# Attention and weight statistics of a four-stage layer kernel: twelve chunk buffers, sums on VectorE, low parts and bias on GpSimd

## The reference, cut to what matters

```python
x = x + _L0_attn_ref(_layernorm(x), Wqkv, bqkv, Wo, bo)
x = x + _L0_ffn_ref(_layernorm(x), w1, mean_w1, w2, mean_w2, w3, mean_w3)
# _L0_attn_ref
qkv = x @ Wqkv + bqkv                      # 512 -> 3 * 128
attn = softmax(q @ k.T / sqrt(128))
out = (attn @ v) @ Wo + bo
# _L0_ffn_ref, each of its three weights is replaced by
d = w - mean_w
W = mean_w + mean(abs(d)) * sign(d)
h = silu(x @ W1.T) * (x @ W3.T);  out = h @ W2.T
```

## Time and profile before

| what | us |
|---|---|
| median of 3 runs | 1560.31 (1559.79 to 1561.89) |
| the profiled execution: its own time | 1560.82 |
| its span from first to last instruction | 1558.9 |
| first stage: up to the first `weff` | 165.16 |
| PE busy over the span | 1348.8 (87%) |
| DVE, ACT, POOL busy | 1146.0, 827.5, 655.3 |

### The profile page before, as it was taken

The page is one execution under the profiler, slowest core; times in us unless marked ns, Lnnn a source line. Parts: engine busy times, 40 slices in busy tenths (PEclk is TensorE's granted clock), DMA queues, the critical chain, the costliest instruction groups (busy, mean ns, idle before and its releaser), DMA issues.

```text
span 1558.9 us, 21230 instructions
## 1 busy us (share of the span) xinstructions
PE 1348.8 (87%) x7142; PEld 1123.2 (72%) x7142; DVE 1146.0 (74%) x2233; ACT 827.5 (53%) x1794; POOL 655.3 (42%) x620
## 2 busy tenths in 40 slices
PE   2875899999778898779465999999999999999977
PEld 1753688888677876667244888888888888888866
DVE  5544433323438899789987999998888998889864
ACT  3575322223225665566333777667766667667741
POOL 3433000000027664555333655555555555666612
PEclk9966799999989999999566999999999999999998
DMA  6543000000021135545650000000000000000011
GB/s 217 170 154 117 0 1 0 1 1 1 11 85 57 53 104 161 161 133 149 201 173 30 12 1 26 26 26 26 26 27 26 26 26 26 26 26 15 12 64 54
DMA packets 83723, 95.59 MB, mean 61 GB/s; under 512 B 11681, under 2 KB 59297, under 8 KB 83105
## 3 DMA queue, kind: packets, MB, share of 16 engines
q1 hardware_dynamic: 83616, 94.24, 19.3%
HBM read 75.34 MB, written 18.87 MB: 60 GB/s over the span
## 4 chain that ended last, share of the span: by engine, by line
PE 65%; DVE 13%; issue 3%; ACT 2%; POOL 2%; DMA 2%; SPq 2%; DVEq 1%; POOLq 0%; ACTq 0%
PE ps L311 15%; PE ps L313 15%; PE ps L312 15%; PE ps L1561 8%; PE ps L1581 3%; PE ps L1580 3%; DVE xn_l L1238 2%; DVE rop L1196 2%; DMA wuvo<-pr_hl 1%; DVE rop L1194 1%; DVE acc L1173 1%; PE ps L1352 1%; DVE pm L1226 1%; PE ps L1473 1%; DVE rop L1195 1%
## 5 line engine op out<-in xcount | busy, mean ns | idle before, releaser
L652 POOL TENSOR_SCALAR pm<-pm,smx 128x128 f32<-128x128 f32 (+7 forms) x256 | 190.2, 752 | 212.1 <-DVE smx L1232 212.1
L899 ACT ACTIVATE pm<-pm,smx 128x128 f32<-128x128 f32 (+7 forms) x256 | 197.2, 772 | 35.1 <-DVE smx L1226 33.4
L1226 DVE CUSTOM_DVE_ANT_0 pm<-ps,mbias 128x128 f32<-128x128 f32 (+7 forms) x256 | 191.5, 753 | 29.1 <-PE ps L313 14.1
L1561 PE MATMUL ps<-ident,pm 128*128 128x128 f32 x1152 | 174.9, 277 | 10.4 <-DVE xn_l L1238 4.9
L905 ACT ACTIVATE xn_h<-ps 128x512 fp32r<-128x512 f32 (+3 forms) x256 | 129.0, 513 | 85.6 <-PE ps L1561 82.7
L1238 DVE TENSOR_TENSOR xn_l<-ps,xn_h 128x512 fp32r<-128x512 f32 (+3 forms) x256 | 144.6, 587 | 26.6 <-ACT xn_h L905 25.7
L311 PE MATMUL ps<-latT_l,qc_h 128*128 128x512 f32 (+3 forms) x384 | 142.6, 371 | 21.5 <-POOLq L302 12.1
L1561 PEld LDWEIGHTS ps<-ident,pm 128*128 128x128 f32 x1152 | 132.0, 141 | 36.7 <-issue 13.3
L1173 DVE SCALAR_TENSOR_TENSOR acc<-relu,iw,acc 128x768 f32<-128x768 f32 (+4 forms) x105 | 119.1, 1175 | 27.0 <-ACT relu L821 26.4
L313 PE MATMUL ps<-latT_h,qc_h 128*128 128x512 f32 (+3 forms) x384 | 134.1, 349 | 0.0
L312 PE MATMUL ps<-latT_h,qc_l 128*128 128x512 f32 (+3 forms) x384 | 133.7, 348 | 0.0
(11 more groups left out here) (248 smaller groups left out, 3815.0 us busy)
## 6 DMA issues: line engine op xcount, KB each, us to landing
iwq_raw<-in_L_attn_idx_wq_w SPq DMA_DIRECT2D x48, 256.0 KB, 3.2
ow_raw<-in_L_attn_o_w SPq DMA_DIRECT2D x16, 512.0 KB, 4.0
wuvo<-pr_hl SPq DMA_DIRECT2D x16, 512.0 KB, 3.5
base<-in_L_ffn_mean_w SPq DMA_DIRECT2D x28, 256.0 KB, 3.0
wring<-in_L_ffn_w SPq DMA_DIRECT2D x24, 256.0 KB, 3.3
wq<-pr_hl SPq DMA_DIRECT2D x16, 256.0 KB, 2.4
wuvo_h<-wuvo SPq DMA_DIRECT2D x16, 256.0 KB, 2.7
wuvo_l<-wuvo SPq DMA_DIRECT2D x16, 256.0 KB, 3.1
```

Source lines behind the costliest of these rows:

```text
L652: pool.tensor_scalar(pm[:, i % 4, 0:w], pm[:, i % 4, 0:w], smx[:, 32 + i:33 + i], 0.0, ALU.mult, ALU.add).then_inc(hd_p, 1)
L899: act.activation(pm[:, i % 4, 0:w], pm[:, i % 4, 0:w], ACT.Exp, bias=smx[:, i:i + 1], scale=-1.0, accum_out=smx[:, 16 + i:17 + i]).then_in ...
L1226: dve.tensor_tensor_reduce(out=pm[:, i % 4, 0:w], in0=two_banks(2 * (i % 2), w), in1=mbias[:, TRI[t]:TRI[t + 1]], scale=1.0, scalar=3.0 * BIG,
L1561: done = pe.transpose(ps[:, 4 + i % 2, tile(k)], pm[:, tq % 4, tile(4 * c + k)], ident[:])
```

## The change

- The ring has up to twelve buffers: the three of `wring` and nine that lie in the back of `base[2]`. For the chunks of w2, whose own mean weights are loaded into `base[2]`, it is six buffers (0, 1, 2, 9, 10, 11), and for the last four chunks 0, 1, 2 and `row_bc` (slot 12). `AFTER` says how many chunks must have been summed and signed before a chunk may be loaded: for chunks 12 to 27 all up to the one twelve earlier; for chunks 28 to 30 25, 26 and 27; for chunks 33 to 39 all up to the one six earlier; for chunks 40 to 43 it is 38, 39, 40 and 40.
- ACT makes only the sign of a chunk (`wt_sgn`). The sum is a `tensor_reduce` with absolute value on DVE (`weight_sums`): 6 behind the first layernorm, one behind each `u`, two behind each `b`, one behind each S, T and Y, and all that are left behind the last Y, ahead of `norm(1,1)`.
- ACT rounds the projection weights and `Wo` (`at_wh`) and the four q and k groups; POOL makes the low parts of the weights, and adds the output bias to x tile by tile ahead of chunks 12 to 19. Every Y step on DVE also waits for `row_free`, which now counts tiles.

The core of the diff:

```diff
+            pool.wait_ge(at_wh, 1)
+            pool.tensor_tensor(wqkv_l[:], raw, f(wqkv_h[:]), ALU.subtract)
+            pool.tensor_tensor(wo_l[:], base[2][:, 2048:2048 + HID], f(wo_h[:]), ALU.subtract).then_inc(at_w, 1)
             for chunk in range(WCHUNKS):
+                if 12 <= chunk < 12 + NT:
+                    t = chunk - 12
+                    pool.wait_ge(ln_xn, t + 1)
+                    pool.tensor_tensor(xt(t), xt(t), row_bc[:], ALU.add).then_inc(row_free, 1)
...
-                act.activation(sgn[m][:, s * width:(s + 1) * width], slot, ACT.Sign)
-                act.drain()
-                act.activation(slot, slot, ACT.Abs, accum_out=absum[:, chunk:chunk + 1])
-                act.drain().then_inc(wt_abs, 1)
+                act.activation(sgn[m][:, s * width:(s + 1) * width], slot, ACT.Sign).then_inc(wt_sgn, 1)
+            raw = base[2][:, 0:NK * 3 * D0].rearrange("p (k n) -> p k n", k=NK)
+            act.wait_ge(ld_a, 80)
+            act.activation(wqkv_h[:], raw, COPY)
+            act.activation(wo_h[:], base[2][:, 2048:2048 + HID], COPY).then_inc(at_wh, 1)
             sqrt(0, NT)
...
+            def weight_sums(n):
+                for _ in range(min(n, len(chunks))):
+                    chunk = chunks.pop(0)
+                    dve.wait_ge(wt_d, chunk + 1)
+                    dve.tensor_reduce(absum[:, chunk:chunk + 1], ring(chunk), AXX, ALU.add, apply_absolute_value=True)\
+                        .then_inc(wt_abs, 1)
             norm(0, 0)
-            split(wqkv_h[:], wqkv_l[:], raw)
-            split(wo_h[:], wo_l[:], base[2][:, 2048:2048 + HID])
-            dve.drain().then_inc(at_w, 1)
-            for t in range(NT):
-                dve.tensor_tensor(xt(t), xt(t), row_bc[:], ALU.add)
-            dve.drain().then_inc(row_free, 1)
+            weight_sums(6)
...
                 else:
                     dve.wait_ge(at_y, i + 1)
+                    dve.wait_ge(row_free, i + 1)
                     dve.scalar_tensor_tensor(xt(i), ps[:, 7 - i % 2, :], sm0[:, 3 * NT + i:3 * NT + i + 1], xt(i),
                                              ALU.mult, ALU.add).then_inc(at_x, 1)
+                    weight_sums(1)
+            weight_sums(WCHUNKS)
             dve.drain()
             norm(1, 1)
```

More of the change, by code:

```diff
@@ L46, with weight_slot @@
 WCHUNKS = 2 * NI + 16
-ROW_FREE = 9
-RING = []
-for _c in range(WCHUNKS):
-    _slot = _c % 3 if _c < ROW_FREE else (_c - ROW_FREE) % 4
-    _users = [_n for _n in range(_c) if RING[_n][0] == _slot]
-    RING.append((_slot, _users[-1] if _users else None, len(_users)))
+RAW_COLS = 2560
+def weight_slot(chunk):
+    if chunk < 2 * NI:
+        slot = chunk % 12
+    elif chunk < 2 * NI + 12:
+        slot = (0, 1, 2, 9, 10, 11)[(chunk - 2 * NI) % 6]
+    else:
+        slot = (0, 1, 2, 12)[(chunk - 2 * NI) % 4]
+    return slot, RAW_COLS + 512 * (slot - 3) if 3 <= slot < 12 else None
+RING, AFTER = [], []
+for _c in range(WCHUNKS):
+    _slot, _col = weight_slot(_c)
+    _taken = [_n for _n in range(_c) if weight_slot(_n)[0] == _slot]
+    if _c >= 2 * NI:
+        _lo, _hi = (_c - 2 * NI) * 448, (_c - 2 * NI) * 448 + 448
+        _taken += [_n for _n in range(_c) if weight_slot(_n)[1] is not None
+                   and weight_slot(_n)[1] < _hi and _lo < weight_slot(_n)[1] + 512]
+    RING.append((_slot, sum(weight_slot(_n)[0] == _slot for _n in range(_c))))
+    AFTER.append(max(_taken) + 1 if _taken else 0)
 TRI = [P * (t * (t + 1) // 2) for t in range(NT + 1)]
@@ L353, in ring @@
         def ring(chunk):
-            slot, width = RING[chunk][0], wt_chunk(chunk)[2]
-            return wring[:, slot, 0:width] if slot < 3 else row_bc[:, 0:width]
+            (slot, col), width = weight_slot(chunk), wt_chunk(chunk)[2]
+            if slot == 12:
+                return row_bc[:, 0:width]
+            return wring[:, slot, 0:width] if slot < 3 else base[2][:, col:col + width]
         def w2_chunk(g):
@@ L392, in _ @@
                     sp.wait_ge(at_w, 1)
[L393 to L397, removed]
+                number = RING[chunk][0]
+                reach(sp, wt_abs, AFTER[chunk])
+                reach(sp, wt_sgn, AFTER[chunk])
+                if number == 12:
+                    sp.wait_ge(row_free, NT)
                 sp.dma_start(dst, ms).then_inc(ld_w[number], 16)
@@ L710, in _ @@
                     act.wait_ge(at_qkv, u - 1)
-                act.activation(xn_t[:, u % 2, :], ps[:, u, :], ACT.Identity,
-                               bias=bq_col[:, u // 2:u // 2 + 1]).then_inc(at_q, 1)
+                bias = bq_col[:, u // 2:u // 2 + 1]
+                act.activation(xn_t[:, u % 2, :], ps[:, u, :], ACT.Identity, bias=bias)
+                act.activation(qkT_h[:, u // 2, 512 * (u % 2):512 * (u % 2) + 512], ps[:, u, :], ACT.Identity,
+                               bias=bias).then_inc(at_q, 1)
                 weight_chunk()
@@ L738, in _ @@
                 weight_chunk()
-            act.drain().then_inc(wt_tot, 1)
             meet(act, 1)
@@ L988, in norm @@
                 dve.drain()
-            norm(0, 0)
-            dve.wait_ge(ld_a, 80)
-            raw = base[2][:, 0:NK * 3 * D0].rearrange("p (k n) -> p k n", k=NK)
-            split(wqkv_h[:], wqkv_l[:], raw)
-            split(wo_h[:], wo_l[:], base[2][:, 2048:2048 + HID])
-            dve.drain().then_inc(at_w, 1)
-            for t in range(NT):
-                dve.tensor_tensor(xt(t), xt(t), row_bc[:], ALU.add)
-            dve.drain().then_inc(row_free, 1)
+            chunks = list(range(WCHUNKS))
+            def weight_sums(n):
[4 more added lines that the diff above has]
+                        .then_inc(wt_abs, 1)
+            norm(0, 0)
+            weight_sums(6)
             for u in range(4):
```

21 lines of the change are left out of this document (13 added, 8 removed).

## The result

| | before | after |
|---|---|---|
| median of 5 runs, us | 1559.79 (1554.98 to 1561.89) | 1570.11 (1566.10 to 1570.97) |
| ratio to before, 95% interval | | 1.0064 (1.0046 to 1.0082) |
| span of the profiled execution | 1558.9 | 1567.3 |
| first `weff` | 165.16 | 175.64 |

The changed kernel is slower by 0.64%, some 10 us; 1568.2 was predicted. One run out of ten of the experiment with the split flush took 2232.65 us at a granted clock of 0.559, where the nine others have about 0.927, and is left out of that experiment's figures. The first `weff` starts 10.5 later.

A forecast was written before the change was run, and what follows sets the result against it. No engine was the bound throughout; a chain from engine to engine was. Terms -3.9 + 2.8 - 1.7 + 1.0 + 1.3 + 9.3 - 0.9 = +7.9 gave span 1566.8, time 1568.2 us; range 1561.5 to 1575.

The forecast's parts named there:

- the front: Stage start up to the projections: they start at 39.1, 3.9 us earlier; bounds 2.2 to 5.3.
- the flush: Between last Y and statistics: the last four chunks' loads wait for sum 38, costing 9.3 us; bounds 8 to 14.
- a subtraction and the rest of a scale, 1.65: First layernorm: each tile's DVE scale waits for POOL, 1.26 + 0.29, with hand-over 1.65 us; seven such steps.
- the port hardly matters: Rival, DVE against POOL: DVE slips in first, projections start near 34.5; +1.7 in all, 1562.0 us; chance 0.13.
- Before the first maximum: After the last v group: DVE's copy and low part wait for POOL, two sums stand ahead; +2.8 us (1.2 to 3.7).
- The 7 us that waiting sums might have added in the periods: Attention periods: six DVE sums would add up to 7 us if they waited for POOL like the scale.
- The periods: Exp 0 to exp 6: 0.9 less on ACT against a DVE sum of 0.61; 0.43 x 4 = 1.7 us gained (0 to 2.5).
- the rival in which ACT is the pace: Attention: both lighter chunks shorten each period, 1.8 us a period, 10.8 over six; 1550.9 us; chance 0.11.
- Between the products with v: ACT's rounding to the second product: exp 7 +4.1 waiting for chunks 29 and 30, 3.1 won back; +1.0 us (-2 to +4).
- The second product and the last Y steps: End of attention: product unchanged; a sum behind each of the first three Y delays the last, +1.3 us.
- The second layernorm: After the attention: it meets only signs on ACT and no POOL; -0.9 us (0 to -2).
- some 2 us either way: PE's clock: where it rises from 1.2 to 2.4 GHz within a product of 24 matmuls shifts, adding this to each forecast.

The follow-up runs named there:

- the experiment with the split flush: Changed kernel with two of the remaining weight sums behind the last Y and four in the second layernorm's tiles; 1562.66 us against 1558.96, ratio 1.0033.
- square root first: Changed kernel with only ACT's square root moved back ahead of its two weight roundings; 1563.33 us against 1559.92, ratio 1.0026.
- the fastest kernel: Changed kernel with POOL held through the first layernorm, period sums behind the maximum, last sums partly in the second layernorm, square root before roundings; 1546.03 us, ratio 0.9917.
- the front alone with POOL held: Kernel before, plus only weight rounding on ACT before its square root, low parts on POOL, first subtraction held for two scales; 1554.10 us, ratio 0.9969.

## Why the prediction was right, and where its terms were off

The mechanism was right: the front gains less than it could, and the flush decides. That the number came so close is partly luck, as the terms show.

- *The front: predicted 3.9 earlier, measured 2.1*, just outside the bounds. The start was well placed: `wqkv_l` took 3.42 (3.5 assumed), the square root ran at 17.44 (17.3). The first scale came at 23.39, 1.8 before my 25.2: behind the end of `wqkv_l` three small ops passed at one instruction of 1.2 each, and I had charged four at 1.4. What failed is the step "a subtraction and the rest of a scale, 1.65" a tile. The six tiles from 26.69 to 38.76 took 2.01 each. Scales of 1.5 to 1.6 and of 0.89 alternate, so a pair of tiles takes the time of three subtractions (4.0) where two of my steps make 3.3. The last tile took 3.5 from its scale to the projections, not 2.3. POOL paid almost nothing: nine subtractions in 12.18 are 1.35 each, against 3.70 / 3 = 1.23 for three.
- *The rival "the port hardly matters"* is refuted in the same rows, and by holding POOL: it put the projections near 34.5, and they came at 34.11 only when POOL was kept out (and ACT's signs with it).
- *Before the first maximum: predicted +2.8, measured +2.5* (from the first score matmul to the maximum 4.92, before 2.47), made of the parts I named: a low part of 1.63 where it had been 0.69, with its copy 0.3 longer, and two sums of 0.60.
- *The sums.* A 512-column sum took 0.6 beside POOL's subtractions as well (69.34, 1.28 for two, while POOL ran five subtractions from 65.95). The Trainium skill ("SBUF — State Buffer", "Who interferes with whom") says so of `tensor_reduce`, and here the trace agrees. The 7 us that waiting sums might have added in the periods could not have come in any case: POOL ran nothing from 80.3 to 104.4, so nearly all sums of the periods met no subtraction.

```profile
65.95 6.85 POOL L556 TENSOR_TENSOR base<-base 128x512 f32<-128x512 f32 x5
```

- *The periods: 5.73 measured, 5.7 predicted; from exp 0 to exp 6 the gain is 1.7 (1.7).* The 0.43 a period that I multiplied by four doesn't follow from my own prices, 0.9 less 0.61. It comes out because a chunk on ACT loses 1.0 (1.52 before, 0.53 now, from the sign to the rounding) and not 0.9, and the sum costs 0.59: luck in this term. ACT's wait for the maximum rose from 0.92 to 2.30: its lighter load became idle time. That refutes the rival in which ACT is the pace; moving a sum behind the maximum then gave 0.59 a period, the length of the sum.
- *The first product with v: -2.1, not priced.* From exp 6 to ACT's rounding it took 7.34 before (101.93 to 109.27) and takes 5.28 now (100.67 to 105.95). 0.6 is the sum that stands behind the product's last input and ahead of exp 6. 1.5 is the clock: the same 24 matmuls take 7.21 and not 8.68, since PE is at its higher level from about the eighth of them on and not only from the fifteenth. The granted clock of the stretch is 0.79, before 0.64.

```profile
100.59 0.79 PE L311 MATMUL ps<-xn_l,v_h 128*128 128x512 f32 x1 [2.15 <-DVE xn_l L1024]
98.74 0.80 PE L329 MATMUL ps<-xn_l,v_h 128*128 128x512 f32 x1 [1.74 <-DVE xn_l L1060]
```

- *Between the products with v: +2.8 (+1.0, bounds -2 to +4).* From the rounding to the second product it took 18.73 before (109.27 to 128.00) and 21.50 now (105.95 to 127.45). Exp 7 came 5.5 later behind the rounding than before (4.1 predicted), with ACT waiting 5.72 and 2.62 for chunks 29 and 30; the lighter chunks behind it won back 2.7 (3.1 predicted).
- *The second product and the last Y steps: +0.5 (+1.3).* The product, "unchanged" in my sum, was 0.5 shorter by the clock (8.12 against 8.64 up to its rounding). The Y steps themselves took 1.0 more (4.30 against 3.31), near the 1.3 predicted.
- *The flush: +11.1 (+9.3, bounds 8 to 14).* The largest term and the one that decided. The first load took 3.3 from issue to POOL (142.80 to 146.10), as in the earlier trace rows. The second, issued 0.9 behind it, took 5.6 (143.71 to 149.35): 3.25 behind the first, not the 1.3 that bandwidth alone gives. Of the four loads of weights one landed 2.9 behind its own issue, the others 5.2 to 5.5. The earlier trace rows had shown this pattern and I had used it only for the bound; four pairs in a burst should have been priced by it.
- *The second layernorm: -0.6 (-0.9).*

The sum was +10.5 for +7.9. Three terms, the front, the part between the products and the flush, came out 1.8 worse than priced each, 5.4 together. The clock in the two products, for which my sum had no term and only a "some 2 us either way" beside it, gave 2.0 back, and the rest of the program ran 2.1 shorter (1391.7 against 1393.7), which nothing in my sum foresaw: the span, 1567.3, lies 0.5 above the 1566.8 of the forecast by that luck. The time, 1570.1, lies 1.9 above the forecast, and 10.3 above the median before.

## What to carry to other kernels

An engine's busy time says nothing of what it costs to give it work: here POOL, fed by deeper buffers, more than doubled the time of DVE's scales where they met, though nobody waited for POOL, and eight additions taken out of an idle stretch of DVE brought nothing. Before a difference in a single trace is put down to an edit, compare a piece of work that the edit leaves alone. When a ring is released by a low-priority step (a sum, a store), place that step by who waits for the buffer: moving one sum of a period from ahead of a maximum to behind one was worth some 8.6 us here, more than half of it because the loads that wait for the sums started before the rounding and not behind it. Start chains of short ops before the long ops of the engine that they meet, even at the price of delaying those.

## What the runs showed of the hardware

- A two-input or scaling op on DVE passes between two of POOL's subtractions even when these run back to back, but can pay for all that is left of the one in hand: 1.69 and 1.15 for eight columns that take 0.17 each when POOL is idle (square root first). The short ops lose most for their length: each of them cost a whole POOL instruction, while the scales cost one only every second time.
- Loads in a burst don't land at even distances: 3.3 us from issue to POOL for the first pair and 5.6 for the second, issued 0.9 later, and the same pattern before (POOL at 141.74 and only at 145.48).
- TensorE's granted clock over the first half of the attention, with the same 103 matmuls, in the table by stretches (columns: stretch, length, PE, weight load, DVE, ACT, POOL, clock, DMA share and GB/s), first of the changed kernel, then of the fastest:

```profile
65.60:106.00 40.40, 26.84 (x103) 20.38 (x103) 25.30 (x41) 18.85 (x34) 13.45 (x11) 0.75 0.27 89
```

```profile
56.28:93.20 36.92, 23.64 (x103) 18.26 (x103) 27.16 (x44) 21.40 (x37) 24.05 (x20) 0.91 0.49 161
```

The mean is 0.75 in the one and 0.91 in the other, between the levels of 1.2 and 2.4 GHz, and the matmuls take 3.2 us less. PE's idle time in the two stretches is nearly the same, 13.6 and 13.3. How much of the fastest kernel's gain is that, and how much the waits themselves, no run here separates.
- The level can differ for the same piece of work with nothing changed near it. The first product with v is 24 matmuls; up to ACT's rounding it took 8.68 in the kernel before, 7.21 in the changed kernel, and 5.90, with the clock at 1.00 from its first matmul, in the front alone with POOL held, whose attention is that of the kernel before. With the fastest kernel it is the same (5.91):

```profile
87.25 0.50 PE L329 MATMUL ps<-xn_l,v_h 128*128 128x512 f32 x1 [1.57 <-DVE xn_l L1063]
```

So up to 2.8 us of a difference in `weff` between two profiled executions can be this, and whether it belongs to a kernel or to an execution no run here shows.
